# Layer 1's contexts and Q weights loaded before the store of the last but one tile of rows

## The reference, cut to what matters

```python
x = x + tanh(g_xattn[0]) * attention0(layernorm(x), ctx, ctx, ...)   # 16 heads of 16
x = x + tanh(g_ffn[0])   * moe(layernorm(x), ...)     # 8 experts, top 2, gelu
x = x + tanh(g_xattn[1]) * attention1(layernorm(x), ctx, ctx, Wq, bq, Wk, bk, Wv, bv, Wo, bo)
x = x + tanh(g_ffn[1])   * quantised_ffn(layernorm(x), ...)
```

## Time and profile before

| | |
|---|---|
| runs | 909.31, 912.82, 913.91 us; median 912.82 |
| the profiled execution | 913.17 us, span 911.5 us |
| TensorE busy | 849.7 us, 93% of the span |
| DVE busy | 621.6 us, 68% |
| ScalarE busy | 501.2 us, 55% |
| POOL busy | 163.7 us, 18% |
| mean granted clock of TensorE | 0.972 of full speed |

### The profile page before, as it was taken

How to read it: one execution, slowest core, us unless ns; L and a number is a source line. 1 busy time by engine, 2 the same in 40 slices (tenths; PEclk the granted TensorE clock), 3 DMA queues, 4 the chain that set the end, 5 groups by cost and what they waited for, 6 DMA issues and landing times.

```text
span 911.5 us, 14427 instructions
## 1 busy us (share of the span) xinstructions
PE 849.7 (93%) x4538; PEld 473.9 (52%) x4539; DVE 621.6 (68%) x1220; ACT 501.2 (55%) x670; POOL 163.7 (18%) x285
## 2 busy tenths in 40 slices
PE   9999999999988999999977899999999979993398
PEld 6543333333457999999844333333333654441387
DVE  5898888888771222233248988888886578698942
ACT  4567777777731222222225577777777684597660
POOL 3241111111264000000063333000005303000000
PEclk9999999999999999999987999999999999997699
DMA  8898465665364111111367864433420000000011
GB/s 285 181 278 239 96 170 165 162 168 136 111 214 145 35 35 35 35 35 35 110 211 183 209 176 85 83 83 82 82 42 2 1 1 0 1 0 0 1 41 52
DMA packets 66576, 91.27 MB, mean 100 GB/s; under 512 B 24151, under 2 KB 50775, under 8 KB 66519
## 3 DMA queue, kind: packets, MB, share of 16 engines
q1 hardware_dynamic: 59212, 67.96, 29.5%
q0 software_dynamic: 5584, 19.93, 6.5%
q10 hardware_dynamic: 1728, 2.75, 0.8%
HBM read 62.77 MB, written 27.44 MB: 99 GB/s over the span
## 4 chain that ended last, share of the span: by engine, by line
PE 80%; DVE 6%; DMA 4%; ACT 3%; SPq 2%; issue 2%; another core or an unknown queue 2%; POOL 1%; DVEq 0%; ACTq 0%; POOLq 0%
PE PS L2123 13%; PE PS L2091 13%; PE PS L2112 12%; PE PS L2282 9%; PE PS L2348 8%; PE PS L2267 8%; PE PS L2369 5%; PE PS L2223 3%; PE PS L2028 2%; PE PS L2051 1%; PE PS L2137 1%; DMA BIG<-MR 1%; PE PS L2074 1%; DMA KSt<-slot_rows 1%
## 5 line engine op out<-in xcount | busy, mean ns | idle before, releaser
L1525 DVE TENSOR_REDUCE MX<-PS 128x1 f32<-128x512 f32 x512 | 321.1, 683 | 44.2 <-PE PS L2091 43.5
L1112 ACT ACTIVATE Pt<-PS 128x1024 f32<-128x1024 f32 x256 | 248.4, 1021 | 103.1 <-PE PS L2112 101.8
L2091 PE MATMUL PS<-KSt,BIG 96*128 96x512 bf16 x512 | 175.0, 385 | 4.8 <-DMA KSt<-qk_parts 2.6
L2112 PE MATMUL PS<-BIG,KSt 99*128 99x512 bf16 x512 | 151.0, 381 | 0.9 <-DMA BIG<-MR 0.9
L2123 PE MATMUL PS<-Pt,VS 128*17 128x512 f32 x1024 | 136.1, 598 | 1.3 <-ACT Pt L1112 1.3
L2091 PEld LDWEIGHTS PS<-KSt,BIG 96*128 96x128 bf16 x512 | 40.5, 97 | 146.9 <-DVE MX L1525 92.9
L2267 PEld LDWEIGHTS PS<-KSt,Pt 128*128 128x128 f32 x736 | 85.6, 192 | 1.7 <-issue 0.7
L2267 PE MATMUL PS<-KSt,Pt 128*128 128x128 f32 x736 | 86.0, 275 | 0.5 <-issue 0.5
L1649 DVE COPY KSt<-PS 128x256 f32<-128x256 f32 x23 | 9.8, 424 | 111.3 <-PE PS L2254 111.3
L2348 PE MATMUL PS<-KSt,BIG 128*128 128x512 f32 x192 | 83.0, 592 | 0.9 <-DVE KSt L1743 0.9
L2112 PEld LDWEIGHTS PS<-BIG,KSt 99*128 99x128 bf16 x512 | 49.8, 98 | 54.5 <-ACT Pt L1112 2.7
(11 more groups left out here) (204 smaller groups left out, 1085.0 us busy)
## 6 DMA issues: line engine op xcount, KB each, us to landing
qk_parts<-BIG SPq DMA_DIRECT2D x64, 192.0 KB
BIG<-in_w POOLq DMA_DIRECT2D x12, 1024.0 KB, 5.7
BIG<-qk_parts SPq DMA_DIRECT2D x32, 192.0 KB, 3.4
KSt<-qk_parts SPq DMA_DIRECT2D x32, 192.0 KB, 3.8
v_rows<-BIG SPq DMA_DIRECT2D x8, 544.0 KB
VS<-v_rows SPq DMA_DIRECT2D x32, 136.0 KB, 3.0
BIG<-qk_parts SPq DMA_DIRECT2D x32, 128.0 KB, 3.9
KSt<-qk_parts SPq DMA_DIRECT2D x32, 128.0 KB, 4.0
```

The costliest lines, as they stand in the source:

```text
L1112: act.activation(PP[:, 2 * (kc % 2) + half, :, :].rearrange("p h t -> p (h t)"), ST[half], ACT.Exp, scale=DK ** -0.5).then_inc(exp_done, 1)
L1525: dve.tensor_reduce(MX[:, g % 2, i % TB, i // TB:i // TB + 1], ring(i), AX.X, ALU.max, negate=True).then_inc(max_taken, 1)
L2091: pe.matmul(ring(i), QS[0:ROWS, g, h, qc * P:(qc + 1) * P], KS[0:ROWS, g, h, :], start=True, stop=True).then_inc(max_done, 1)
L2112: last = pe.matmul(ST[half][:, i * S:(i + 1) * S], KS[0:ROWS + PARTS, g, h, kc * P:(kc + 1) * P], QS[0:ROWS + PARTS, g, h, :], start=True, ...
```

## The change

In SP's program the wait and the four loads stand one tile earlier, ahead of the store of tile 21 in place of tile 22, and the wait is for `w1_staged` of the last tile (its block of W1 copied out of `BIG`) in place of `h_done` of the last tile. Nothing else is changed.

```diff
             t = SLOT_TILES - 1
             load_slots(t // 2, t % 2, t)
             for t in range(SLOT_TILES - 3, SLOT_TILES):
-                if t == SLOT_TILES - 1:
-                    sp.wait_ge(h_done, 2 * SLOT_TILES)
+                if t == SLOT_TILES - 2:
+                    sp.wait_ge(w1_staged, SLOT_TILES)
                     load_context(sp, 1, 1)
                     load_weight(sp, 1, 0, awq_in)
                     load_context(sp, 1, 2)
                     load_context(sp, 1, 3)
                 store_results(t // 2, t % 2)
```

## The result

The changed kernel takes 915.38 us (913.93 to 917.12, 10 runs), the kernel before 909.86 us (905.80 to 913.91, 10 runs, two of the three shown ahead of the prediction being its slowest). The ratio is 1.0062, 95% interval 1.0043 to 1.0080: slower, where 909.5 us was forecast. Ratios leave out one execution of e13, which took 2196 us. The profiled execution of the changed kernel took 915.74 us, span 914.1 us.

What follows compares the result with a forecast made beforehand. TensorE's chain, broken behind the turning of rows by late signals beside the gathers, was taken to bound the kernel. Removed waits 0, moved issues 0, chain -3.3 took the median of 912.82 to 909.5 us, range 904.5 to 915.5.

Steps and rivals of the forecast that it cites:

- What bounds the kernel there, and who waits: Behind the expert stage: the store waits 5.4 us behind loads, POOL waits for its landing, nobody waits for the contexts.
- The store of tile 21: SP's store, still issued at 446.2, was taken to land at 449, between bounds of 447.9 and 451.6.
- The 5.9 us taken for the latest landing of a load: SP's moved loads: landing 5.9 us after issue at the latest, so by 447.4, bounding the store of tile 21.
- The last late signal ... can arrive at 474.6 ... 3.3 us sooner.: TensorE's last late signal to ScalarE comes sooner with the gathers, limited by the product ending at 475.02; chance 0.38.
- The chain's term of -3.3 us: The sum's only nonzero term: TensorE's chain after the expert stage shortens 3.3 us, bounds 0 and 12.27.
- The row at 459.58: ScalarE's row in the earlier trace: with four gathers issued, TensorE's completions showed no lateness yet.
- the slower rival: Earlier gathers make K of the second context late, costing 3.3 us: 916.1 us; chance 0.14.
- More goes than one signal: The whole pattern of late signals moves 3.7 us forward and the clock stays up: 906.3 us; chance 0.22.
- Nothing moves: Stores and gathers at 460 to 478 cause the lateness, or the 26 ns rule holds: 912.8 us; chance 0.26.
- the rule of some 26 ns: The skill's matmul completion signal time; by it signals cannot be 3 us late and moving gathers brings nothing.
- The base: Median of the kernel before, 912.82 us, from which the 3.3 us were taken; the profiled execution was 913.17.
- The pieces of 12.27 us in its chain: Behind the turning of rows: three chain pieces without known releaser, 2.92, 5.83 and 3.52 us, the gain's upper bound.

Runs made afterwards that it cites:

- e13: The changed kernel itself, measured again beside later runs on one chip: 917.14 us, ratio to the kernel before 1.0072.
- e4: The changed kernel without the 16 gathers, DVE adding what lies in the buffer without waiting: 903.48 us, ratio to before 0.9927.
- e14: The kernel before, unchanged, profiled a second time; that one execution took 905.93 us.
- e1: The changed kernel with POOL's gathers held until TensorE has made V of the first context: 908.69 us, ratio to before 0.9998.
- e2: The kernel before with the wait and four loads behind the store of tile 22 instead of ahead: 914.96 us, ratio 1.0071.
- e7: The changed kernel with each of the 16 gathers replaced by a plain 128 KB transfer by POOL: 905.52 us, ratio to before 0.9946.
- e3: The changed kernel, pausing after eight gathers until ScalarE copied the turned rows, low parts of first Q four gathers later: 908.25 us, ratio 0.9978.
- e9: The changed kernel, pausing after eight gathers until ScalarE copied the turned rows, low parts of first Q six gathers later: 905.51 us, ratio 0.9955.
- e15: The changed kernel pausing behind the twelfth gather until ScalarE copied the turned rows, low parts of first Q before the last two: 909.81 us, 0.9992.
- e12: e9 once more, the same split of the changed kernel's gathers, in another set: 904.18 us, ratio to before 0.9986.
- e16: e10 without its wait: the changed kernel with only POOL's low parts of first Q ahead of the last two gathers: 915.79 us, 1.0067.
- e10: e9 with the pause behind the twelfth gather in place of the eighth, low parts before the last two: 903.79 us, ratio to before 0.9980.
- e5: The changed kernel storing a quarter of layer 1's values for two contexts, its attention reading layer 0's values: 916.78 us, ratio to before 1.0080.
- e8: The kernel before with gathers split as in e3, pausing after eight for ScalarE's copies of the turned rows: 910.02 us, ratio 0.9994.

## Why the prediction was wrong

**What bounds the kernel there, and who waits**: right. The store of tile 22 was late behind the loads, POOL waited for it, nobody waited for the contexts. The issue of the loads, both stores, the 1.7 us of landing and the 3.7 us of the gathers came as forecast. The store of tile 21 landed in 2.2 us (forecast 2.8). The 5.9 us taken for the latest landing of a load is the median of two; the later one took 6.2. Nothing hangs on it.

**"The last late signal ... can arrive at 474.6 ... 3.3 us sooner."** This is the step that failed. It moved one signal, the last, by the end of the gathers, and left all the rest of TensorE's stage as it was. But the work that a row holds is given by what TensorE finishes while it runs. Before, the turned rows were done 8.5 us into the row and got through 1.5 and 5.0 us late; after, they are done 12.2 us into it and wait for the row's end. The queries of the first batch hang on them. The wait before the copies grew from 2.93 and 2.94 to 12.74 us, and the products for Q that follow began at half the clock, and took 5.62 us where e4 needs 3.67 at the full clock. So the last product for Q was taken 479.43 - 448.30 = 31.1 us behind the issue of the last store, in place of 478.34 - 449.73 = 28.6: 2.5 us later, where 3.3 sooner was forecast. The chain's term of -3.3 us measured +5.5 in the medians.

The loss is smaller than the 11 us by which the copy moved against e14 (24.7 against 13.7 us behind the issue of the last store). By the first scores 6.4 us of it are left. The likely reason is that the kernel before pays for its own hold later, in e14 at K of the third context (2.92 us) and at the next turned rows; this is argued from the profiles and no run isolates it.

What the runs show is that the start of the gathers decides (e1, e2), that the indirect row is needed (e4, e7) and that breaking it frees the signal (e3, e9, e15). Why some signals in a row get through and others not stays open, and so does the condition without which nothing is held.

**The row at 459.58** The earlier trace rows was read as "no lateness yet" with four gathers issued. That was a hint that lateness may depend on how far the row has run. It was used only to price the slower rival, not to ask which completions would lie further into the row after the move.

**The slower rival** had the direction and nearly the size (3.3 us, against 5.5), by luck, since it had the wrong place: it put the new lateness on K of the second context, which ScalarE took on time (L958 waited 3.03 and 1.03 us in the changed kernel, as before). **More goes than one signal** had the whole pattern move forward with the gathers; the copies came later instead.

**Nothing moves / the rule of some 26 ns** (the Trainium skill, TensorE: Matmul & The Clock Gate, "The cost: per-tile semaphore tail"): where no gathers run, nothing speaks against the rule: in e4 both signals of the turning are recorded within 0.02 us of the modelled ends of their halves. Beside the row of gathers ScalarE's copy came 10.6 us behind that end, and the rule can't price it.

**The base**: the median of before was taken as 912.82 us from three runs; ten gave 909.86. That 915.38 us lies inside the stated range, up to 915.5, is owed to this base, 3 us too high: the measured ratio on a base of 912.82 gives 918.5. The profile, at 913.17 us, was an execution with much lateness. The pieces of 12.27 us in its chain were one draw of a thing that varies from run to run (44.5 and 48.3 us from the last store to the first scores in two profiles), and a theory of what the change does to them needed more than one profile.

## What to carry to other kernels

When a change lets a transfer stream of another engine start sooner, ask for both ends of the stream, and list by name each completion on the critical path that falls inside it before and after. Where an idle engine waits for work that is already done, with an unknown releaser, price a move into that stretch by the whole length of the stream, and take several profiles first, from more than one set of executions. If a long row of indirect gathers must run beside a dependent chain, try to break it at the point where the chain's next completion is due; here a pause behind eight gave a ratio to before of 0.9955 in place of 1.0062 (e9 against the changed kernel), and nothing clear in the set without holds (e12, 0.9986).

## What the runs showed of the hardware that was not expected

- Beside an unbroken row of POOL's indirect gathers (one issued each 1.25 us) completions of TensorE reached ScalarE up to 10.9 us late (e16) and DVE up to 11.6 us late (e2). In all nine profiles with 12 or 16 in a row, outside the set of e10 to e12, held signals came out 3.3 to 4.2 us behind the row's last gather. The wait for the first turned rows was 12.1 to 13.0 us with 16 in the row (after, e2, e5, e13, e16) and 7.1 us with 12 (e15); with 8 they came on time (e3, e9), or up to 1.5 us late in e8.
- Held signals are released in TensorE's order, 0.06 us apart (e2, 474.08 to 474.20).
- 16 plain transfers of the same size in place of the gathers (8.64 us of issues) held nothing, and neither did the stores of values and of parts alone (e4). Making the first two stores of values a quarter changed nothing (e5).
- In one set of executions (e10 to e12) nothing was held, an unbroken row of 16 included, and no signal was missing from the traces; in all others with gathers TensorE's signals came late, from some 1 us (e3, e9) up, and 126 to 222 of the 256 landing signals of the gathers were missing. Whether the recording causes the holds, or both have one cause, is open.
- Also open: where in a row a hold begins, and whether a row that is as slow as the gathers but not indirect holds too. Layer 0's scatters, which are indirect too, have small waits of the same kind beside them (1.7 us before L1619 in the changed kernel), and breaking that row was not tried.
- A 128 KB store issued by SP right behind 1792 KB of its loads landed in 5.4 us, alone in 1.7 us; one issued 4.1 us behind the last of the loads landed in 2.2 us.
